# Attention and FP4 feed-forward block: rounding and block reciprocals of h and x in one instruction each, high scales and row factor on ScalarE

## The reference

```python
xn = _layernorm(x, axis=-1)
x = x + _L0_attn_ref(xn, W_qkv, W_out) + _L0_ffn_ref(xn, w_gate, w_up, w_down)
```

```python
def fp4_quant_dequant(x):
    xb = x.reshape(shape[:-1] + (shape[-1] // BLOCK, BLOCK))
    scale = jnp.max(jnp.abs(xb), axis=-1, keepdims=True) / 6.0
    scale = jnp.maximum(scale, jnp.float32(1e-12))
    xn = xb / scale
    idx = jnp.searchsorted(_MID, jnp.abs(xn))
    q = _GRID[idx] * jnp.sign(xn) * scale
    return q.reshape(shape)
...
    gate = fp4_linear(x, w_gate)
    y = fp4_linear(x, w_up)
    h = jax.nn.silu(gate) * y
    return fp4_linear(h, w_down)
```

## Time and profile before

| What | Value |
|---|---|
| median of 3 runs | 1552.2 us (1551.77 to 1552.58) |
| profiled execution, its own time | 1554.58 us |
| its span, first to last instruction | 1552.8 us |
| VectorE busy | 1498.1 us (96%), 5042 instructions |
| TensorE busy | 1385.2 us (89%), weight loads 949.7 us (61%) |
| ScalarE busy | 771.6 us (50%) |
| GpSimd busy | 173.2 us (11%) |
| mean granted TensorE clock | 0.986 of full speed |
| HBM | 24 GB/s over the span |

### The profile page before, as it was taken

How to read it: one execution, slowest core, us unless ns; L and a number is a source line. 1 busy time by engine, 2 the same in 40 slices (tenths; PEclk the granted TensorE clock), 3 DMA queues, 4 the chain that set the end, 5 groups by cost and what they waited for, 6 DMA issues and landing times.

```text
span 1552.8 us, 42501 instructions
## 1 busy us (share of the span) xinstructions
PE 1385.2 (89%) x10702; PEld 949.7 (61%) x10702; DVE 1498.1 (96%) x5042; ACT 771.6 (50%) x2072; POOL 173.2 (11%) x541
## 2 busy tenths in 40 slices
PE   0169999999999999999999999999999999999996
PEld 0146666666666666666666666666666666666664
DVE  5859999999999999999999999999999999999996
ACT  1775445555454544455454545454554545454541
POOL 1521010101001010101001010101010010101000
PEclk9969999999999999999999999999999999999998
DMA  5003233332333333333323333332333232323223
GB/s 110 4 8 66 58 63 66 71 69 55 78 67 68 62 75 68 61 69 68 72 55 78 65 65 65 74 68 58 71 66 77 52 78 65 66 63 75 62 50 70
DMA packets 293240, 100.00 MB, mean 64 GB/s; under 512 B 258272, under 2 KB 292704, under 8 KB 293216
## 3 DMA queue, kind: packets, MB, share of 16 engines
q1 hardware_dynamic: 293216, 99.73, 30.7%
HBM read 19.99 MB, written 16.78 MB: 24 GB/s over the span
## 4 chain that ended last, share of the span: by engine, by line
DVE 54%; issue 34%; DVEq 7%; ACT 2%; PE 1%; SPq 1%; DMA 0%; POOL 0%; ACTq 0%; POOLq 0%
DVE q_rows L858 4%; DVE osum L895 4%; DVE hw L820 4%; DVE xblk L753 3%; DVE h L739 3%; DVE drec L713 2%; DVE xw L838 2%; DVE hv L802 2%; DVE hq L830 2%; DVE xq_s L871 2%; DVE hu L824 2%; DVE c_row L883 1%; DVE xblk L772 1%; DVE att L718 1%; DVE qsh L681 1%
## 5 line engine op out<-in xcount | busy, mean ns | idle before, releaser
L550 ACT ACTIVATE att_t<-trp 128x256 f16<-128x256 f32 x256 | 98.1, 383 | 357.7 <-PE trp L1105 353.2
L1150 PE MATMUL outp<-w_down_cat,q_rows 128*128 128x256 f16 x1408 | 247.0, 274 | 0.0
L534 ACT ACTIVATE qexp<-qsh,c_q 128x256 f32<-128x256 f32 x128 | 65.0, 508 | 226.5 <-DVE qsh L681 226.5
L398 POOL TENSOR_TENSOR var_scaled<-squares,var_mul 128x1 f32<-128x1 f32 x128 | 24.5, 192 | 1246.8 <-ACT scratch L488 1239.8
L1150 PEld LDWEIGHTS outp<-w_down_cat,q_rows 128*128 128x128 f16 x1408 | 138.7, 98 | 16.7
L1152 PE MATMUL outp<-w_down_lo,q_rows 128*128 128x256 f16 x640 | 148.4, 275 | 0.0
L513 ACT ACTIVATE xnt<-trp 128x256 f16<-128x256 f32 x256 | 96.6, 377 | 57.4 <-PE trp L1045 57.4
L746 DVE TENSOR_REDUCE hblk<-h 128x44 f32<-128x704 f32 x128 | 123.9, 968 | 0.1
L802 DVE TENSOR_TENSOR hv<-h,hblk 128x704 f32<-128x704 f32 x128 | 112.8, 881 | 0.0
L1019 PE MATMUL unit1a<-w_gate,xqt 128*128 128x352 f16 x256 | 80.5, 314 | 32.9 <-DVE qsh L681 31.5
L1019 PE MATMUL unit0a<-w_gate,xqt 128*128 128x352 f16 x256 | 80.5, 314 | 32.4 <-DVE qsh L681 31.5
(11 more groups left out here) (213 smaller groups left out, 4399.5 us busy)
## 6 DMA issues: line engine op xcount, KB each, us to landing
xring<-x SPq DMA_DIRECT2D x128, 128.0 KB, 2.7
out<-xring SPq DMA_DIRECT2D x128, 128.0 KB, 2.5
xqt<-xq_s SPq DMA_TRANSPOSE x128, 2.4
q_rows<-q_rows SPq DMA_TRANSPOSE x128, 3.5
raw_qkv<-wqkv_t SPq DMA_DIRECT2D x1, 768.0 KB, 7.8
raw_gate<-wgate SPq DMA_DIRECT2D x8, 88.0 KB
raw_up<-wup SPq DMA_DIRECT2D x8, 88.0 KB
raw_down<-wdown SPq DMA_DIRECT2D x1, 704.0 KB, 6.3
```

The costliest lines, as they stand in the source:

```text
L550: nc.scalar.activation(att_t[:, par, part, :], tr32, ACT.Copy).then_inc(att_split, 1)
L1150: nc.tensor.matmul(downp, hqt[:, par, m, :], w_down_cat[:, m, :], start=(m == 0), stop=False)
```

## The change

On VectorE, the block scales of h and x now lie side by side in one tile `blk` of 60 columns, and the values to be rounded in tiles `hx_v`, `hx_w`, `hx_u`, `hx_q` of 960 columns (704 of h, 256 of x). One reciprocal over 60 columns replaces one over 44 and one over 16. Each of the three rounding passes is one instruction over 960 columns (`round_hx`) and replaces one over 704 and one over 256. `xs_hi`, `hs_hi` and `c_row` are made on ScalarE, by three new ACTIVATEs in `scales_x` and `scales_h`, placed ahead of `exp_q`; the low parts `xs_lo` and `hs_lo` stay on VectorE, in `low_scales`, and wait for ScalarE. The h scales carry another power of two, so that h and x share the constant of the second pass, which `h_floor` and `c_d` make up for. VectorE's order follows: the x multiplication moves ahead of `shift_q`, the low scales behind `gate_h`, and parts 1 and 2 of the attention change places with their neighbours. Semaphore counts are renumbered throughout.

```diff
@@ -135,27 +135,23 @@
...
-        xblk = sb("xblk", [P, 3, XB])
+        blk = sb("blk", [P, 3, FB + XB])
+        hblk, xblk = blk[:, :, 0:FB], blk[:, :, FB:FB + XB]
...
-        hu = sb("hu", [P, F], fp16)
-        hq = sb("hq", [P, F], u16)
+        hx_v = sb("hx_v", [P, F + D])
+        hx_w = sb("hx_w", [P, F + D], u16)
+        hx_u = sb("hx_u", [P, F + D], fp16)
+        hx_q = sb("hx_q", [P, F + D], u16)
         hq_s = q_flat[:, 0:4 * F].rearrange("p (t k) -> p t k", t=2)
         hqt = q_flat[:, 4 * F:4 * F + 2 * HT * P].rearrange("p (t m k) -> p t m k", t=2, k=P)
...
@@ -558,11 +555,30 @@
                 nc.scalar.activation(th[:, half, :], unit[(par + half) % 2][0][:, 0:FH], ACT.Tanh, scale=c_g[:, :])\
                     .then_inc(tanh_done, 1)
 
+            def scales_x(t):
+                if not is_tile(t):
+                    return
+                act.wait_ge(xq_step, after(t, 6, 2))
+                nc.scalar.activation(xs_hi[:, :].rearrange("p (b i) -> p b i", i=2), twice(xblk[:, 1, :]), ACT.Copy)\
+                    .then_inc(x_scaled, 1)
+
+            def scales_h(t, par):
+                if not is_tile(t):
+                    return
+                act.wait_ge(hq_step, after(t, 9, 5))
+                if begun(t - 2):
+                    act.wait_ge(o_step, after(t - 2, 2))
+                nc.scalar.activation(c_row[:, par, :], hrow[:, 1, :], ACT.Copy, scale=c_d[:, :]).then_inc(h_scaled, 1)
+                nc.scalar.activation(hs_hi[:, :].rearrange("p (b i) -> p b i", i=2), twice(hblk[:, 1, :]), ACT.Copy,
+                                     scale=hrow[:, 2, :]).then_inc(h_scaled, 1)
+
             def step(n, d):
                 k, par, odd = 2 * n + d, d, 1 - d
                 split_att(k - 1, odd, 0)
                 exp_k(k + 1, odd)
                 split_att(k - 1, odd, 1)
+                scales_x(k + 2)
+                scales_h(k - 1, odd)
                 exp_q(k + 1, odd)
                 tanh_gate(k, 0, par)
                 split_xnt(k + 2, par, 0)
...
@@ -753,135 +769,114 @@
                 nc.vector.tensor_reduce(xblk[:, 0, :], xn[:, par, :].rearrange("p (b j) -> p b j", j=BL), AX.X, ALU.max,
                                         apply_absolute_value=True).then_inc(xq_step, 1)
 
-            def block_scales(t, par, u, upar):
-
-
-
-
+            def hx_after(u, nth):
+                return u * 4 + nth
+
+            def block_scales(t, u):
                 do_h, do_x = is_tile(t), is_tile(u)
                 if do_x:
-                    dve.wait_ge(xq_step, after(u, 8, 1))
+                    dve.wait_ge(xq_step, after(u, 6, 1))
                     nc.vector.tensor_scalar(xblk[:, 1, :], xblk[:, 0, :], SIX_TIE * 2.0 ** 11, XS * TINY * 2.0 ** 11, ALU.mult, ALU.max)\
                         .then_inc(xq_step, 1)
                 if do_h:
-                    dve.wait_ge(hq_step, after(t, 14, 1))
-                    nc.vector.tensor_scalar(hblk[:, 1, :], hblk[:, 0, :], SIX_TIE, h_floor[:, :], ALU.mult, ALU.max)\
+                    dve.wait_ge(hq_step, after(t, 9, 1))
+                    nc.vector.tensor_scalar(hblk[:, 1, :], hblk[:, 0, :], SIX_TIE * 2.0 ** 11, h_floor[:, :], ALU.mult, ALU.max)\
                         .then_inc(hq_step, 1)
-                if do_x:
-                    dve.wait_ge(xq_step, after(u, 8, 2))
-                    nc.vector.reciprocal(xblk[:, 2, :], xblk[:, 1, :]).then_inc(xq_step, 1)
+                    dve.wait_ge(hq_step, after(t, 9, 2))
+                    nc.vector.tensor_reduce(hrow[:, 0, :], hblk[:, 1, :], AX.X, ALU.max).then_inc(hq_step, 1)
+                if do_h or do_x:
+                    if do_x:
+                        dve.wait_ge(xq_step, after(u, 6, 2))
+                    both = slice(0 if do_h else FB, FB + XB if do_x else FB)
+                    nc.vector.reciprocal(blk[:, 2, both], blk[:, 1, both]).then_inc(hx_step, 1)
                 if do_h:
-                    dve.wait_ge(hq_step, after(t, 14, 2))
-                    nc.vector.tensor_reduce(hrow[:, 0, :], hblk[:, 1, :], AX.X, ALU.max).then_inc(hq_step, 1)
-                if do_h:
-                    nc.vector.reciprocal(hblk[:, 2, :], hblk[:, 1, :]).then_inc(hq_step, 1)
-                    dve.wait_ge(hq_step, after(t, 14, 3))
+                    dve.wait_ge(hq_step, after(t, 9, 3))
                     nc.vector.tensor_scalar(hrow[:, 1, :], hrow[:, 0, :], 2.0 ** -23, None, ALU.mult)\
                         .then_inc(hq_step, 1)
-                if do_x:
-                    nc.vector.tensor_copy(xs_hi[:, :].rearrange("p (b i) -> p b i", i=2), twice(xblk[:, 1, :])).then_inc(xq_step, 1)
-                if do_h:
-                    dve.wait_ge(hq_step, after(t, 14, 5))
-                    nc.vector.reciprocal(hrow[:, 2, :], hrow[:, 1, :]).then_inc(hq_step, 1)
-                if do_x:
-                    dve.wait_ge(xq_step, after(u, 8, 4))
+
+            def row_scale(t):
+                if not is_tile(t):
+                    return
+                dve.wait_ge(hq_step, after(t, 9, 4))
+                nc.vector.reciprocal(hrow[:, 2, :], hrow[:, 1, :]).then_inc(hq_step, 1)
+
+            def over_scales_h(t, par):
+                if not is_tile(t):
+                    return
+                dve.wait_ge(hx_step, hx_after(t + 3, 1))
+                rows = lambda ap: ap.rearrange("p (o b i) -> p o b i", b=FB, i=2)
+                nc.vector.tensor_tensor(rows(hx_v[:, 0:F]), rows(h[:, par, :]), pairs_of(hblk[:, 2, :]), ALU.mult)\
+                    .then_inc(hq_step, 1)
+
+            def over_scales_x(t, par):
+                if not is_tile(t):
+                    return
+                dve.wait_ge(hx_step, hx_after(t, 1))
+                nc.vector.tensor_tensor(hx_v[:, F:F + D].rearrange("p (o b i) -> p o b i", b=XB, i=2),
+                                        xn[:, par, :].rearrange("p (b o i) -> p o b i", b=XB, i=2),
+                                        pairs_of(xblk[:, 2, :]), ALU.mult).then_inc(xq_step, 1)
+
+            def round_hx(t, u, part):
+                do_h, do_x = is_tile(t), is_tile(u)
+                if not do_h and not do_x:
+                    return
+                both = slice(0 if do_h else F, F + D if do_x else F)
+                if part == 0:
+                    if do_h:
+                        dve.wait_ge(hq_step, after(t, 9, 6))
+                    if do_x:
+                        dve.wait_ge(xq_step, after(u, 6, 3))
+                    nc.vector.tensor_scalar(hx_w[:, both], hx_v[:, both].bitcast(u16)[:, 1:2 * (both.stop - both.start):2], 1, None,
+                                            ALU.bitwise_or).then_inc(hx_step, 1)
+                if part == 1:
+                    dve.wait_ge(hx_step, hx_after(u, 2))
+                    nc.vector.tensor_scalar(hx_u[:, both], hx_w[:, both].bitcast(bf16), 2.0 ** -3, None, ALU.mult)\
+                        .then_inc(hx_step, 1)
+                if part == 2:
+                    dve.wait_ge(hx_step, hx_after(u, 3))
+                    if begun(t - 1):
+                        dve.wait_ge(hq_step, after(t - 1, 9))
+                    if begun(u - 1):
+                        dve.wait_ge(xq_step, after(u - 1, 6))
+                    nc.vector.tensor_scalar(hx_q[:, both], hx_u[:, both].bitcast(u16), GRID16, -GRID16, ALU.add, ALU.add)\
+                        .then_inc(hx_step, 1)
+
...
+            def low_scales(t, u):
+                if is_tile(u):
+                    dve.wait_ge(x_scaled, after(u))
                     nc.vector.tensor_tensor(xs_lo[:, :].rearrange("p (b i) -> p b i", i=2), twice(xblk[:, 1, :]),
                                             xs_hi[:, :].rearrange("p (b i) -> p b i", i=2), ALU.subtract).then_inc(xq_step, 1)
-                if do_h:
...
-            def row_factor(t, par):
-                if not is_tile(t):
-                    return
-                dve.wait_ge(hq_step, after(t, 14, 7))
-                nc.vector.scalar_tensor_tensor(hs_lo[:, :].rearrange("p (b i) -> p b i", i=2), twice(hblk[:, 1, :]), hrow[:, 2, :],
-                                               hs_hi[:, :].rearrange("p (b i) -> p b i", i=2), ALU.mult,
-                                               ALU.subtract).then_inc(hq_step, 1)
-                if begun(t - 2):
-                    dve.wait_ge(o_step, after(t - 2, 2))
-                nc.vector.tensor_scalar(c_row[:, par, :], hrow[:, 1, :], c_d[:, :], None, ALU.mult)\
-                    .then_inc(c_row_done, 1)
+                if is_tile(t):
+                    dve.wait_ge(h_scaled, after(t, 2))
+                    nc.vector.scalar_tensor_tensor(hs_lo[:, :].rearrange("p (b i) -> p b i", i=2), twice(hblk[:, 1, :]), hrow[:, 2, :],
+                                                   hs_hi[:, :].rearrange("p (b i) -> p b i", i=2), ALU.mult,
+                                                   ALU.subtract).then_inc(hq_step, 1)
 
...
@@ -905,28 +900,26 @@
```

(25 more changed lines are left out.)

83 lines of the change are left out of this document (20 added, 63 removed).

## The result

| | before | after |
|---|---|---|
| median of runs on the same chip | 1551.99 us (4 runs, 1551.68 to 1552.58) | 1640.31 us (4 runs, 1638.81 to 1641.29) |
| after / before | | 1.0568, 95% interval 1.0549 to 1.0586 |
| profiled execution, span | | 1640.38 us, 1638.7 us |

The account below looks back on a forecast made before the run. VectorE, never idle at 11.245 us a step, was taken as the bound; savings of 0.24 + 0.12 + 0.21 = 0.57 us over 125 steps, 71 us, gave 1481 us from a median of 1552.2, range 1464 to 1503.

Parts of the forecast that it names:

- the paragraph on ScalarE: Three small ACTIVATEs ahead of exp(q), taken at 0.3 us each, two waiting for the row's reciprocal, all hidden by idle time.
- the 1.77 us of idle time before exp(q): ScalarE's wait for VectorE's shifted q in the kernel before, claimed to hide the three new ACTIVATEs.
- this cover: ScalarE's idle time before exp(q); without it exp(q), tanh and the split of x would be late, and TensorE with them.
- Two of the signs: Signs of being wrong: VectorE waiting for ScalarE or TensorE, a fused pass of 1 us, exp(q) directly behind the three ACTIVATEs.
- rival "slower": VectorE's fused passes fall from the fast to the ordinary rate: 1.4 us lost a step, 1727 us; chance 0.05.
- Block scales, 0.93 for the stretch: VectorE, x scale to maximum of q: 1.39 us becomes 0.93, or 1.15 with instructions run later; 0.24 us a step saved.
- Row factor, 0.12: c_row leaves VectorE: 0.12 us a step saved.
- Rounding, 0.21: VectorE's three x passes go (0.48 us), the widened h passes cost 0.27: 0.21 us a step saved.
- Sum 0.57: VectorE's savings of 0.24, 0.12 and 0.21 us a step: 11.245 to 10.675, 71 us over 125 steps.
- ScalarE's own prices: The three new ACTIVATEs of 32, 1 and 88 columns, each between nothing and 0.51 us, taken as 0.3.
- The bound that the prediction called covered: Three ACTIVATEs at 0.51 us each, 1.53 us, claimed to fit ScalarE's 1.77 us of idle time.
- Who comes next, TensorE at 10.43: TensorE's own need of 10.43 us a step, below VectorE's 10.675, puts the end of all gains at 1450 us.

Follow-up runs that it names:

- four row factors: The changed kernel with c_row in four buffers in place of two, so ScalarE waits for the output sum one tile older: 1480.49 us, ratio 0.9534.
- the one with the row factor later: The changed kernel, two buffers and wait kept, with the row factor's ACTIVATE moved behind the splits of x: 1479.01 us, ratio 0.9530.

## Why the prediction was wrong

**The step that failed is the paragraph on ScalarE.** It named what the new ACTIVATEs wait for as the row's reciprocal, and called them "hidden by the 1.77 us of idle time before exp(q)". The first of the two h instructions, the row factor, waits for one thing more, the output sum of tile k-3 (`o_step`), by the diff in `scales_h`. In the prediction that wait doesn't occur, so it stands in its sum at nothing; it cost 160 us, 1.27 us a step by the trace. Its price was knowable from the order: the second half of `add_up` stands between the second and the third pass, well behind the shift of q, so the row factor could not start before it was done, and exp(q) not before the row factor and the high scales, though the shifted q was there long before. From rows of before that sum could have been made: shift, pass 1, output sum, pass 2, add, c_row, hs_hi, exp(q), tanh, against passes and sums alone on VectorE. The text even had the right question, "if this cover were gone, exp(q), the tanh and the split of x queued behind it would be late", and answered it only for the wait that it had seen.

The wait costs 160 us in the changed kernel (against four row factors) and 113 us in the kernel before. Both runs, and the one with the row factor later, show it from three sides. Two of the signs that the prediction had named for being wrong were there: VectorE waited for ScalarE, and exp(q) started directly behind the three. The rival "slower" of the prediction, which has the direction right, a loss of the fast rate, is refuted: the fused passes read 0.65, 0.40 and 0.39 above, against forecasts of about 650, 400 and 400 ns.

**Block scales, 0.93 for the stretch: measured 0.96** (1006.70 to 1007.66 in the version with four row factors). h scales 0.28 for 0.29; maximum 0.12 for 0.08; reciprocal 0.43 for 0.43; product 0.01 for 0.01. The Trainium skill says in "VectorE: DVE Perf Modes", section "The DRAIN you can't avoid", that a semaphore behind each instruction costs nothing extra, as measured on eight copies. For a short instruction with a direct reader the rows disagree: the reader, which waits for the semaphore, starts 0.28 behind the h scales' start, another instruction 0.16. Whether the semaphore or the reading costs this is not separated.

**Row factor, 0.12: 0.10. Rounding, 0.21: 0.195.** Sum 0.57: (1552.4 - 1480.5) / 125 = 0.575. The single figures here add up to less than that. Start distances, averaged from 600 to 1200 us of the traces, close the gap: 0.12 for the row factor, 0.21 for the rounding, and 0.25 for the block scales with what was moved out of their stretch, since the row's reciprocal takes 0.07 for a forecast 0.10 and the low x scales 0.10 for 0.12. Two changes that nobody forecast cancel: the snapshot takes 0.06 less with its new neighbours and the second gate product 0.05 more. So the sum was right by its terms. That it came out to the microsecond, with small misses both ways, is luck.

**ScalarE's own prices** were forecast at 0.3 each, and are 0.22, 0.28 and 0.36. The Trainium skill, "ScalarE: Activation LUTs", section "What ACT_TABLE_LOAD costs", gives figures from which an estimate is 0.21, 0.28 and 0.35, and the trace agrees. Its advice to keep products on VectorE doesn't hold here as long as ScalarE has room, since the row factor is worth 12.5 us away from VectorE.

**ScalarE's room, "the 1.77 us": too large, without harm here.** What ScalarE does later in the step feeds TensorE, which feeds ScalarE's next step. This circle doesn't get shorter by the change, while the step does. So the room shrinks by the gain itself, 0.57, beside the 0.56 that the three ACTIVATEs take from start to start (0.30 for the first two, 1008.36 to 1008.66, and 0.26 for the third): 1.77 less both is 0.64, and 0.62 is what the version with four row factors has left. The bound that the prediction called covered, 1.53 us for the three, is 0.67 more than their 0.86, and would just have fitted into that version's 0.72.

**Who comes next, TensorE at 10.43: 10.40.** With the wait gone, 1480 us stand 35 us above that end.

Still open is why some instructions follow the power-of-two product after 0.01 and others after 0.10 to 0.12, and why the output sum follows the h scales after 0.30 to 0.41. The best complete versions measured, 1475 to 1480 us, lie no further apart than these distances.

## What to carry to other kernels

When a step moves from one engine to another, list every wait that it takes along, and for each ask when in the new engine's step its releaser runs and what stands behind it in the queue; a wait that cost nothing in one queue, where its releaser had always run, cost 160 us in the middle of another. The last reader of a buffer that is reused after two tiles is such a releaser, though no data comes from it. And before you fill an engine's idle time, count it from start to start, take off what the step itself will get shorter, and ask of everything queued behind it who waits for it already: 0.92 us of extra work in 0.72 us of room cost 0.16 us a step, through the split of x and not through the tanh that had been watched.

## What the runs showed of the hardware that had not been expected

- The start of an instruction depends on the one behind it by more than data. The power-of-two product (0.10 us long) takes 0.01 ahead of the maximum of q, 0.12 ahead of the h multiplication and 0.10 ahead of the output sum.
- Behind the same h scales, the output sum started 0.30 us after them in one parity of tiles and 0.41 in the other; the profile counts 0.17 of the latter as issue.
- Durations depend on neighbours. The maximum over the h scales took 0.16 us with a reciprocal ahead of it, 0.20 directly behind its source, and 0.19 with the maximum of q between them, so it is not the nearness of the source alone; the distance to its successor was 0.08, 0.12 and 0.10. The snapshot (128x544) took 0.71 before and 0.66 in the version with four row factors.
- TensorE's granted clock stayed at 1.00 in the stretch of the changed kernel, although TensorE was busy for 175.59 us of 200 and stood still for up to 1.8 us at a time.
